# A scan spread over four accumulator banks, with its row load split and its projection work re-laid

## What is computed

```python
xz = silu(einsum('oc,bchw->bohw', in_proj_w, x) + in_proj_b)
x_ssm, res, gate = split(xz, 3, axis=1)
xf = silu(depthwise_conv3(x_ssm) + dw_b)
x_h = gather(xf, perm)                       # per head: tokens in scan order
dt, B_t, C_t = gather(softplus/linear(dbc_w @ xf), perm)
h_t = exp(dt*A) * h_(t-1) + dt*B_t * x_t     # a scan over 1024 tokens, 8 states, 2 heads
y_t = <C_t, h_t> + D * x_t
y = gather(y, inverse perm)
x = x + silu(out_proj_w @ (y * silu(gate) + res) + out_proj_b)
```

## Time and profile before

| | |
|---|---|
| median of 3 runs | 1748.39 us (1747.06 to 1748.44) |
| the profiled execution, whole | 1750.19 us |
| its span, first to last instruction | 1748.4 us |
| PE busy | 1651.4 us (94%) |
| DVE, ACT, POOL busy | 1147.0, 892.9, 413.1 us |
| mean granted TensorE clock | 0.984 of full speed |

### The profile page before, as it was taken

One profiled execution on the slowest core, in us unless ns is written; L12 is line 12 of the kernel. 1 busy time (PEld: TensorE's weight loads), 2 busy tenths in 40 slices (PEclk: granted clock), 3 DMA queues, 4 the chain that ended last, 5 costly groups with the idle time before them and its releaser, 6 DMA issues.

```text
span 1748.4 us, 24401 instructions
## 1 busy us (share of the span) xinstructions
PE 1651.4 (94%) x8693; PEld 927.0 (53%) x8693; DVE 1147.0 (66%) x2472; ACT 892.9 (51%) x1091; POOL 413.1 (24%) x423
## 2 busy tenths in 40 slices
PE   4689899999999999999999999999999999999988
PEld 3254554555545655456545565455554565545643
DVE  6878776557855676647865568565775576662775
ACT  4647353565355654455634645356525555445542
POOL 0304311044021331133220341204402142113220
PEclk9889999999999999999999999999999999999999
DMA  6203410134102331223211341023410233112301
GB/s 207 94 0 103 145 28 13 73 127 145 40 25 89 114 118 40 74 92 105 95 21 73 127 139 34 14 85 120 140 40 36 84 117 109 40 48 75 102 25 49
DMA packets 124078, 140.16 MB, mean 80 GB/s; under 512 B 52259, under 2 KB 101475, under 8 KB 123950
## 3 DMA queue, kind: packets, MB, share of 16 engines
q1 hardware_dynamic: 109902, 103.18, 18.6%
q0 software_dynamic: 12288, 34.68, 5.9%
q10 hardware_dynamic: 1760, 0.64, 0.2%
HBM read 78.46 MB, written 60.01 MB: 79 GB/s over the span
## 4 chain that ended last, share of the span: by engine, by line
PE 64%; DVE 10%; issue 9%; POOL 9%; DMA 4%; ACT 3%; SPq 0%; DVEq 0%; POOLq 0%; ACTq 0%
PE bank L1618 61%; POOL d_scan L463 6%; DMA rows<-d_y,rank 1%; POOL rows L480 1%; DVE bn L913 1%; DMA d_y<-buf_b 1%; PE bank L1786 1%; POOL work L469 1%; DVE gate L1136 1%; PE bank L1917 1%; PE bank L1837 1%; DVE res L1260 1%; DVE res L1258 1%; DMA rows<-d_scan 1%; ACT res L643 1%
## 5 line engine op out<-in xcount | busy, mean ns | idle before, releaser
L1618 PE MATMUL bank<-buf_a,win_hi 128*128 128x512 f16 x1536 | 461.9, 383 | 8.2 <-DVE buf_a L985 8.1
L1618 PE MATMUL bank<-buf_a,win_lo 128*128 128x512 f16 x768 | 293.6, 382 | 0.0
L1618 PE MATMUL bank<-buf_b,w_hi 128*128 128x512 f16 x960 | 288.1, 382 | 2.3 <-DVE buf_b L985 2.3
L1618 PEld LDWEIGHTS bank<-buf_a,win_hi 128*128 128x128 f16 x1536 | 149.5, 99 | 174.5 <-DVE buf_a L985 10.9
L463 POOL DMA_INDIRECT d_scan<-rows,rank x128 | 125.3, 979 | 347.3 <-ACT rows L648 304.7
L1618 PE MATMUL bank<-buf_b,w_lo 128*128 128x512 f16 x480 | 183.2, 382 | 0.0
L1618 PE MATMUL bank<-buf_a,w_hi 128*128 128x512 f16 x576 | 171.3, 379 | 1.4 <-DVE x_odd L1228 1.3
L1618 PEld LDWEIGHTS bank<-buf_b,w_hi 128*128 128x128 f16 x960 | 94.0, 99 | 112.5 <-DVE buf_b L985 3.0
L480 POOL DMA_INDIRECT rows<-d_y,rank x128 | 125.8, 983 | 97.8 <-DMA d_y<-buf_b 61.6
L1618 PEld LDWEIGHTS bank<-buf_a,win_lo 128*128 128x128 f16 x768 | 75.7, 99 | 92.4 <-issue 3.0
L1618 PE MATMUL bank<-gate,w_out 128*128 128x512 f32 x256 | 120.2, 602 | 1.1 <-DVE gate L1341 1.1
(11 more groups left out here) (253 smaller groups left out, 3068.9 us busy)
## 6 DMA issues: line engine op xcount, KB each, us to landing
rows<-d_scan SPq DMA_DIRECT2D x16, 1092.0 KB, 5.8
d_y<-buf_b SPq DMA_DIRECT2D x64, 256.0 KB, 2.2
work<-in_x SPq DMA_DIRECT2D x24, 512.0 KB, 4.5
d_gram<-rows SPq DMA_DIRECT2D x32, 260.0 KB, 2.4
x_even<-in_x SPq DMA_DIRECT2D x16, 512.0 KB, 5.5
x_odd<-in_x SPq DMA_DIRECT2D x16, 512.0 KB, 5.4
out_x<-x_even SPq DMA_DIRECT2D x16, 512.0 KB, 3.1
out_x<-x_odd SPq DMA_DIRECT2D x16, 512.0 KB, 2.6
```

The source lines that it names most:

```text
L1618: return eng.matmul(out, lhsT, rhs, start=start, stop=stop, skip_group_check=True, **kw)
```

## The change

It changes which bank holds what, what SP loads in which pieces, and the order of work on PE, ACT and DVE around the scan. No product, copy or vector operation is added or dropped. The only new instructions are 16 more DMA issues.

1. `scan_y` uses four banks, 3 to 6, one for each pair of chunks, and its waits for emptied banks go. Both heads now use the same banks for factors and increments. On ACT the first copy of head 0's output stands ahead of head 1's first exponential, and the others between the exponentials.
2. Each head's row load is two transfers: the 17 columns of dt, B and C first (1024 rows of 68 bytes, semaphore `scanrows`), then the 256 columns of x (semaphore `scanx`, which PE waits for ahead of the increments).
3. On PE head 0's sums come after 17 units of the input projection and not after 18. `tokens(3)` comes one quarter unit later.
4. On DVE the blocks of head 0 come ahead of the masks of head 1, and the bound of the scan's output behind the states of head 1.
5. Of the six quarter units between head 1's inner products and its output, two stay. Twelve (units 21, 22 and 23) stand behind the scan, four ahead of the first transposes, four between the halves, and four behind. The product that carries the bound stands within head 1's `scan_y`.
6. The first parts of the output projection are in another order, for the new banks.

```diff
-        yt_bank = ((5, 6), (3, 4), (3, 3), (4, 4))
-        dh_bank = lambda h, c: ((3, 4, 0, 0), (5, 6, 0, 0))[h][c // 2]
-        m_bank = (5, 3)
-        factor_bank = ((3, 5), (5, 3))
-        in_bank = (3, 4, 6, 1, 2, 1, 2, 1, 2, 1, 4, 5, 6, 3, 2, 1, 4, 5) + (2, 1) * 3
-        out_bank = (0, 1, 2, 5, 6, 0, 3, 4)
+        yt_bank = ((3, 5), (4, 6), (3, 3), (4, 4))
+        dh_bank = lambda c: (3, 4, 0, 0)[c // 2]
+        m_bank = 5
+        factor_bank = (3, 5)
+        in_bank = (3, 4, 6, 1, 2, 1, 2, 1, 2, 1, 4, 5, 6, 3, 2, 1, 4) + (2, 1) * 3 + (2,)
+        out_bank = (0, 2, 1, 5, 6, 0, 3, 4)
...
-                    eng.dma_start(rows4[:, h], d_scan[h].rearrange("(c p) r -> p c r", p=P)).then_inc(s[f"scanrows{h}"], 16)
+                    stored = d_scan[h].rearrange("(c p) r -> p c r", p=P)
+                    eng.dma_start(rows4[:, h, :, DH:ROW], stored[:, :, DH:ROW]).then_inc(s[f"scanrows{h}"], 16)
+                    eng.dma_start(rows4[:, h, :, 0:DH], stored[:, :, 0:DH]).then_inc(s[f"scanx{h}"], 16)
...
+                scan_y(0, 0)
                 scan_exp(1, 0)
+                scan_y(0, 1)
                 scan_exp(1, 1)
-                scan_y(0, 0)
+                scan_y(0, 2)
                 scan_exp(1, 2)
-                scan_y(0, 1)
                 scan_decays(1)
-                scan_y(0, 2)
                 scan_y(0, 3)
                 scan_factors(1)
-                filler(3)
+                filler(2)
                 for j in range(4):
                     scan_y(1, j)
+                filler(1)
...
                 scan_factors(m, 0, z)
+                scan_blocks(m, 0)
                 scan_masks(m, 1)
-                scan_blocks(m, 0)
...
                 scan_blocks(m, 1)
+                scan_states(m, 1)
                 y_largest(m)
-                scan_states(m, 1)
                 y_scale(m)
...
                 tokens(2)
-                filler(1)
+                piece(KC + 1)
                 tokens(3)
-                filler(5)
+                piece(5 * KC - 1)
                 if not (first or last):
                     gn_sum(m + 1, 0)
-                filler(4)
+                filler(3)
...
-                        if j >= 2:
-                            wait(eng, "y_ev", m, 4 * h + j - 1)
-                        out = ps[3 + j % 2][:, (c % 2) * DH:(c % 2 + 1) * DH]
+                        out = ps[3 + j][:, (c % 2) * DH:(c % 2 + 1) * DH]
...
                 scan_inner(1)
-                wait(eng, "w_maxc", m, ROUNDS + 1)
-                eng.transpose(bound_row, y_bound[:, 7:8], ident).then_inc(s["w_maxt"], 1)
-                piece(6)
-                wait(eng, "w_maxr", m, 2 * ROUNDS + 3)
-                mm(bound_all, const("ones")[0:1, :], y_bound[0:1, 1:2], True, True).then_inc(s["w_maxb"], 1)
-                scan_y(1)
+                piece(2)
+                scan_y(1, bound_across)
...
-                for n in range(4):
-                    y_chunk(*gate_order[n])
+                piece(4)
+                y_chunk(0, 0)
+                wait(eng, "w_maxr", m, 2 * ROUNDS + 3)
+                mm(bound_all, const("ones")[0:1, :], y_bound[0:1, 1:2], True, True).then_inc(s["w_maxb"], 1)
+                y_chunk(1, 0)
+                piece(4)
+                y_chunk(0, 1)
+                y_chunk(1, 1)
                 piece(4)
                 wait(eng, "in_evac", m, 23)
...
-                for k in (0, 1):
-                    wait(eng, "y_lo", m, k + 1)
-                    out_part(0, k)
-                    out_part(2, k)
-                    out_part(3, k)
+                wait(eng, "y_lo", m, 1)
+                out_part(0, 0)
                 wait(eng, "in_evac", m, 24)
                 out_part(1, 0)
+                out_part(2, 0)
+                wait(eng, "y_gate", m, 3)
+                wait(eng, "y_lo", m, 2)
+                out_part(0, 1)
                 out_part(1, 1)
+                out_part(2, 1)
+                out_part(3, 0)
+                out_part(3, 1)
                 y_chunk(2, 0)
```

More of the change, by code:

```diff
@@ L701, in image @@
                     eng.wait_ge(s["p_rank"], HEADS)
-                    filler(4)
+                    filler(3)
                 else:
-                    filler(9)
+                    filler(8)
                 def scan_decays(h):
@@ L718, in scan_factors @@
                         wait(eng, "fac_tp", m, 4 * h + half + 1)
-                        act(pT[:, half * HALF:(half + 1) * HALF], ps[factor_bank[h][0] + half][:, :], ACT.Copy,
+                        act(pT[:, half * HALF:(half + 1) * HALF], ps[factor_bank[0] + half][:, :], ACT.Copy,
                             scale=const("keep")[:, h:h + 1]).then_inc(s["fac_ptq"], 1)
@@ L722, in scan_factors @@
                         wait(eng, "fac_tp", m, 4 * h + half + 3)
-                        act(qT[:, half * HALF:(half + 1) * HALF], ps[factor_bank[h][1] + half][:, :], ACT.Copy).then_inc(s["fac_ptq"], 1)
+                        act(qT[:, half * HALF:(half + 1) * HALF], ps[factor_bank[1] + half][:, :], ACT.Copy).then_inc(s["fac_ptq"], 1)
                 def scan_y(h, j):
                     wait(eng, "y_mm", m, 4 * h + j + 1)
-                    act(yscan[:, h, 2 * j:2 * j + 2, :], ps[3 + j % 2][:, :].rearrange("p (c d) -> p c d", c=2),
+                    act(yscan[:, h, 2 * j:2 * j + 2, :], ps[3 + j][:, :].rearrange("p (c d) -> p c d", c=2),
                         ACT.Copy).then_inc(s["y_ev"], 1)
@@ L1552, in whole_chunks @@
                     c = slice(half * HALF, (half + 1) * HALF)
-                    TT(mmat[:, c], ps[m_bank[h] + half][:, :], diag[:, c], ALU.add).then_inc(s["m_ev"], 1)
+                    TT(mmat[:, c], ps[m_bank + half][:, :], diag[:, c], ALU.add).then_inc(s["m_ev"], 1)
                 if h == 0:
@@ L1827, in factor_rows @@
                     if h == 0 and a == 0:
-                        wait(eng, "in_evac", m, 18)
+                        wait(eng, "in_evac", m, 17)
                     if h and a == 0:
-                        wait(eng, "h_st", m, 7)
-                        wait(eng, "m_ev", m, 2)
+                        wait(eng, "y_ev", m, 2)
                     if h and a == 1:
@@ L1846, in state_products @@
                             wait(eng, "fac_ptq", m, 4 * h + 1 + c // 2)
+                        if c == 0:
+                            wait(eng, f"scanx{h}", m, 16)
                         if c == 4 and h == 0:
@@ L1865, in scan_inner, with bound_across, scan_y @@
                     state_products(h, range(4, NT - 1))
-                def scan_y(h):
+                def bound_across():
+                    wait(eng, "w_maxc", m, ROUNDS + 1)
+                    eng.transpose(bound_row, y_bound[:, 7:8], ident).then_inc(s["w_maxt"], 1)
+                def scan_y(h, between=None):
                     r = rows4[:, h]
                     for c in range(NT):
+                        if c == NT - 2 and between:
+                            between()
                         j = c // 2
@@ L1898, in image @@
                 scan_inner(1)
-                wait(eng, "w_maxc", m, ROUNDS + 1)
-                eng.transpose(bound_row, y_bound[:, 7:8], ident).then_inc(s["w_maxt"], 1)
-                piece(6)
-                wait(eng, "w_maxr", m, 2 * ROUNDS + 3)
-                mm(bound_all, const("ones")[0:1, :], y_bound[0:1, 1:2], True, True).then_inc(s["w_maxb"], 1)
-                scan_y(1)
+                piece(2)
+                scan_y(1, bound_across)
                 def y_chunk(k, half):
-                    if k == 0 and half == 0:
-                        wait(eng, "h_st", m, 7 * HEADS)
-                    if k == 1 and half == 0:
-                        wait(eng, "y_ev", m, 4 * HEADS)
+                    if k < 2:
+                        wait(eng, "y_ev", m, 4 + 2 * half + k + 1)
                     wait(eng, f"y_in{k // 2}{half}", m, 8 * NT)
                     if k >= 2:
-                        wait(eng, "y_gate", m, (2, 4, 5, 6)[2 * half + k - 2])
+                        wait(eng, "y_gate", m, (1, 2, 5, 6)[2 * half + k - 2])
                     for t in range(4 * half, 4 * half + 4):
```

16 lines of the change are left out of this document (8 added, 8 removed).

## The result

The changed kernel took 1732.18 us (median of four runs, 1731.63 to 1733.98), against 1747.72 us for the kernel before on the same chip: a ratio of 0.9904, 95% interval 0.9887 to 0.9921. It is 15.5 us faster, where 27.0 were forecast.

The account below looks back on a forecast made before the run. PE, busy nearly all the time, was taken to bound the kernel, so only its waits could be won: 30.8 + 3.3 - 3.2 - 3.2 - 0.7 = 27.0 us, giving 1721.4 us; forecast 1716 to 1727, range up to 1736.

Parts of the forecast that it names:

- What was to go: PE's waits in head 0's output (13.6), first transposes (3.4), third pair's gathered rows (10.6), before tokens(3) (3.2): together 30.8 us.
- The low clock of the earlier trace: Granted clock 0.59 and 0.56 after waits in the fifth and seventh images; removing both stretches was to give 3.3 us.
- I take no wait: Second pair of transposes: head 0's gathered rows land at 25.1 us, 2.7 after last issue; PE comes at 27.5.
- rival (b): Waits return: head 1's output chain a microsecond longer, or head 0's gather late beside next image's load; 1729 to 1733, chance 0.20.
- The table load: 1.28 us on ACT behind its first copy, in the chain to head 1's output, where PE waits some 0.4 an image.
- The row load: Short load of dt, B and C before head 0's sums: lands in 3 us instead of 5.8, so no PE wait.
- rival (a): Short-row load no faster than the full one; PE waits for masks, 7 x 1.65 = 11.6 us, giving 1733; chance 0.10.
- The two small terms: New PE waits at head 1's output and behind the first output part: 0.4 us an image, 3.2 in all, each.
- rival (c): No new wait at all and the first image gains its share: 34.1 us gained, so 1714; chance 0.08.

Follow-up runs that it names:

- the last experiment: Twelve quarter units all moved behind the two pairs of transposes, against the kernel whose first exponential of head 1 precedes ACT's first copy (1716.0 us): 1762.3 us, ratio to before 1.0062.
- the kernel with the table load hidden: One line of the changed kernel moved: ACT's first exponential of head 1, with its table load, ahead of the first copy of head 0's output: 1716.01 us, ratio 0.9798.

## Why the prediction was right in direction and too high in gain

**What was to go is gone.** The wait within head 0's output, the first transposes and the wait ahead of the token products are gone, and so is the third pair's wait for gathered rows. In the third image PE comes to the second pair at 27.45 us after the start of head 0's output (619.22 less 1.35 and 0.17), forecast 27.5. The low clock of the earlier trace rows is gone: from 345 to 1587 us the granted clock of the changed kernel is 1.00. That the quarter units are the cover of the second pair is shown by the last experiment: with them behind, the kernel takes 46 us more. Not tried by themselves were the sums one unit sooner and DVE's new order.

**The term that failed** is the one that the prediction put as "I take no wait" at the second transposes. The last issue at 22.4 and PE's arrival were right. What failed was the 2.7 us to landing, the median of other gathers, those at the end of head 1. The last gather of head 0 takes some 3.6 without the load, so the room was 1.5 us and not 2.4, and beside the load it took 6.4. That is 3.7 more than 2.7, 0.9 of it without the load, against 2.4 of room, and so 1.3 us of wait. In all 10.4 listed and 7 x 0.17 of drain are 11.6 us, where 27.0 - 15.5 = 11.5 were missing; that the two agree so well is partly luck, as the other terms were off too (below). It is the second half of rival (b), and the time fell in its range. Two experiments show both ends of it: with the load held back the wait goes (all but 0.7 us) though the gather is issued as late, and with the gather issued 1.4 us sooner it goes though the load stays.

**The table load** was seen, and it stands in the prediction's sums for head 1's output and for the gather's last issue alike. It was priced at head 1's output alone, at 0.4 us an image; that measured 0.26 in the third image (from 14.25 to 13.99 us with the line moved). That it also used up 1.4 us of the gather's room, through the queues of DVE and POOL, was the larger price, and the prediction put it at nothing because it took the room that was left for enough. The row at 592.36 shows 1.28 us with the activation right behind it. The Trainium skill (ScalarE: Activation LUTs, What ACT_TABLE_LOAD costs) puts a switch at 2.66 us with a drain. No trace here shows the drain, and the measured 1.28 is what counts.

**The row load** was forecast at 3 us and took 2.4, so rival (a) was wrong. What the full load would cost was sized at 1.65 us in seven images, 11.6 in all; in the changed kernel it measured 30.6 us in the span, since the wait was 2.5 and the clock fell behind six of the seven.

**The two small terms** were right in kind: the wait behind the first output part is the forecast 0.4 us, by 0.39 in the intervals.

**One term was missing.** In the last image a wait that stands in the kernel before as well, 1.8 us for `st`, was followed in the profiled execution by low clock:

```profile
1666.60:1669.60 3.00, 3.00 (x8) 1.44 (x7) 2.00 (x10) 0.00 (x0) 0.58 (x1) 0.59 0.00 0
1669.60:1672.60 3.00, 3.00 (x12) 1.50 (x11) 0.74 (x1) 1.55 (x2) 0.00 (x0) 0.84 0.00 0
```

The two stretches lost 1.2 and 0.5 us. By the spans the gain is 16.3 us; 27.0 - 11.6 - 1.7, and 1.1 more for head 1's output (8 times 0.4 less 0.26), make 14.8, and the other 1.5 was not traced. Without the wait the forecast would have been too low: the kernel with the table load hidden gains 34.9 us by the spans, near rival (c)'s 34.1. Of the 7.9 above 27.0 it saves 3.2 by the chain to head 1's output, which PE doesn't wait for there; the rest was not traced. The kernel with the table load hidden has the same wait (1.76 against 1.77) and a clock of 1.00 behind it. What decides there is open; nothing was tried on it.

The gather's wait varies from 1.15 to 1.87 us between images, and why it does was not followed further.

## What to carry to other kernels

When a wait is removed, ask of each transfer behind it which other transfer now starts beside it, and of each time to landing which transfers it was read from: here 2.7 us, the median of others, stood for one that takes 3.6 without the load and took 6.4 beside it. An engine's idle time ahead of a wait is where a table load belongs; moved behind the wait, its price can turn up two queues on, in the work that stands behind a late instruction of another engine. If a change removes one wait in two ways, try each way alone, since the second may add only its cost.

## What the runs showed of the hardware

A small indirect gather slows much when a large load begins beside it: the last eighth of head 0's rows took 3.2 to 4.7 us with the load held back until it had landed, 4.2 to 5.3 when the load followed 0.8 us behind its issue, and 6.3 to 6.9 when it had begun some 0.2 us ahead. The Trainium skill (DMA: Bandwidth & Descriptors, Queues, rings and completion order) says that each DMA engine takes turns between its queues, a packet at a time. The trace agrees in so far as both kinds of transfer go on at once while the DMA share is 1.00 (from 614 to 616 us in the changed kernel); how they share an engine it doesn't show. A load of 1024 pieces of 68 bytes took only 2.4 us, and one of the whole rows 5.8.

The granted clock fell to 0.50 behind waits of 2.20 to 3.10 us at the sums and not behind one of 1.64. The length of a wait alone does not decide: a wait of 1.76 or 1.77 us in the last image had either outcome, one of 2.84 us was followed by no fall, and in the kernel before the clock fell behind 1.97 us in the fifth image but not behind 1.98 in the second:

```profile
395.07 0.67 PE L1618 MATMUL bank<-rows,work 128*128 128x256 f32 x2 [1.98 <-ACT buf_b L727]
```

```profile
395.07:400.07 5.00, 5.00 (x27) 4.21 (x28) 4.83 (x24) 3.12 (x7) 0.00 (x0) 1.00 0.47 159
```
